# Cross-attention on one core: a hint instruction for the closing branch of the batch loop on every engine

## What is computed

```python
Q = (q @ Wq + bq).reshape(b, s, H, DH).transpose(0, 2, 1, 3)
K = (k @ Wk + bk).reshape(b, s, H, DH).transpose(0, 2, 1, 3)
V = (v @ Wv + bv).reshape(b, s, H, DH).transpose(0, 2, 1, 3)
scores = jnp.einsum('bhqd,bhkd->bhqk', Q, K) / jnp.sqrt(jnp.float32(DH))
scores = scores * mask
attn = jax.nn.softmax(scores, axis=-1)
ctx = jnp.einsum('bhqk,bhkd->bhqd', attn, V)
ctx = ctx.transpose(0, 2, 1, 3).reshape(b, s, H * DH)
x = q + ctx @ Wo + bo
out = (x - mean(x)) * rsqrt(var(x) + LN_EPS) * gamma + beta
```

## Time and profile before

| | us |
|---|---|
| median of 3 runs | 2252.9 (2248.44 to 2253.84) |
| the profiled execution, its own time | 2253.91 |
| its span, first to last instruction | 2252.1 |
| PE busy | 2119.7 (94%) |
| DVE busy | 1933.0 (86%) |
| ACT busy | 1782.9 (79%) |
| POOL busy | 1038.0 (46%) |

### The profile page before, as it was taken

The page is one execution under the profiler, slowest core; times in us unless marked ns, Lnnn a source line. Parts: engine busy times, 40 slices in busy tenths (PEclk is TensorE's granted clock), DMA queues, the critical chain, the costliest instruction groups (busy, mean ns, idle before and its releaser), DMA issues.

```text
span 2252.1 us, 46384 instructions
## 1 busy us (share of the span) xinstructions
PE 2119.7 (94%) x12348; PEld 886.9 (39%) x12348; DVE 1933.0 (86%) x4283; ACT 1782.9 (79%) x3809; POOL 1038.0 (46%) x1576
## 2 busy tenths in 40 slices
PE   2699999999999999999999999999999999999985
PEld 1234444444444344444444444443444434444432
DVE  6779988898988898888989888898988888988882
ACT  3579798887969879697887969788796978879781
POOL 2116263463726436273543726355372634537234
PEclk8799999999999999999999999999999999999997
DMA  6359789697887969789697868969697896968783
GB/s 219 70 118 177 161 155 206 129 191 142 174 182 145 197 131 187 152 168 195 130 196 141 184 145 171 194 133 194 142 183 157 159 203 129 192 140 176 143 157 87
DMA packets 1117594, 363.28 MB, mean 161 GB/s; under 512 B 1073504, under 2 KB 1073504, under 8 KB 1117408
## 3 DMA queue, kind: packets, MB, share of 16 engines
q1 hardware_dynamic: 1114288, 361.58, 78.2%
q10 hardware_dynamic: 3120, 0.01, 0.1%
HBM read 76.30 MB, written 16.78 MB: 41 GB/s over the span
## 4 chain that ended last, share of the span: by engine, by line
PE 75%; issue 8%; POOL 7%; DVE 6%; ACT 2%; DMA 1%; POOLq 0%; DVEq 0%; ACTq 0%; SPq 0%
PE fill_ps L396 17%; PE fill_ps L397 16%; PE fill_ps L398 16%; PE score_ps L449 13%; PE ctx_ps L470 11%; POOL raw L1199 3%; DVE score_ps L923 2%; ACT probs L621 1%; DVE p L937 1%; POOL bk_scaled L1215 1%; DVE small L805 1%; POOL neg_max L1222 1%; DVE k L952 1%; ACT p L635 1%; POOL cT L1205 1%
## 5 line engine op out<-in xcount | busy, mean ns | idle before, releaser
L621 ACT ACTIVATE probs<-score_ps,neg_max 128x512 f32<-128x512 f32 x1024 | 695.8, 693 | 187.3 <-POOL neg_max L1222 181.7
L923 DVE CUSTOM_DVE_ANT_0 score_ps<-score_ps,mask_sb,small 128x512 f32<-128x512 f32 x1024 | 723.6, 753 | 93.6 <-PE score_ps L449 89.6
L635 ACT ACTIVATE p<-probs,inv_sum 128x512 f16<-128x512 f32 x1024 | 675.0, 724 | 132.9 <-DVE inv_sum L931 92.2
L937 DVE SCALAR_TENSOR_TENSOR p<-probs,inv_sum,p 128x512 f16<-128x512 f32 x896 | 677.6, 792 | 47.9 <-issue 38.1
L1222 POOL TENSOR_SCALAR neg_max<-row_max 128x2 f32<-128x2 f32 x512 | 142.4, 278 | 681.1 <-DVE row_max L923 664.7
L449 PE MATMUL score_ps<-k,q 64*128 64x512 f16 x3072 | 397.8, 380 | 15.3 <-ACT probs L621 8.9
L470 PE MATMUL ctx_ps<-pT,v 128*64 128x512 f16 x3072 | 359.8, 384 | 18.6 <-DMA pT<-p 15.6
L1228 POOL TENSOR_SCALAR down_sum<-row_sum 128x4 f32<-128x4 f32 x256 | 67.9, 265 | 393.9 <-ACT probs L621 385.5
L470 PEld LDWEIGHTS ctx_ps<-pT,v 128*64 128x64 f16 x3072 | 165.7, 110 | 205.4 <-issue 72.5
L449 PEld LDWEIGHTS score_ps<-k,q 64*128 64x128 f16 x3072 | 129.9, 94 | 263.8 <-ACT probs L621 80.9
L396 PE MATMUL fill_ps<-wv,cT 128*128 128x512 f16 x512 | 197.4, 385 | 31.6 <-DVE k L952 25.8
(11 more groups left out here) (91 smaller groups left out, 2992.0 us busy)
## 6 DMA issues: line engine op xcount, KB each, us to landing
raw<-in_xt SPq DMA_DIRECT2D x64, 256.0 KB, 3.2
raw<-in_ct SPq DMA_DIRECT2D x64, 256.0 KB, 3.2
mask_sb<-in_mask_Bx1xSxS_fk SPq DMA_DIRECT2D x64, 256.0 KB, 3.2
acc<-in_x SPq DMA_DIRECT2D x64, 256.0 KB, 3.0
out<-acc SPq DMA_DIRECT2D x64, 256.0 KB, 2.4
pT<-p SPq DMA_TRANSPOSE x512, 4.5
wq_staged<-in_L_xattn_Wq SPq DMA_DIRECT2D x4, 512.0 KB, 7.1
wk_staged<-in_L_xattn_Wk SPq DMA_DIRECT2D x4, 512.0 KB, 10.7
```

The source lines that it names most:

```text
L621: nc.scalar.activation(probs[:, i % E_TILES, :], score_ps[:, i % 4, :], ACT.Exp, bias=neg_max[:, p % 2, i:i + 1], accum_out=row_sum[:, p % ...
L635: nc.scalar.activation(p16[:, q, a, 0, :], probs[:, i % E_TILES, :], ACT.Copy, scale=inv_sum[:, p % 2, i:i + 1]).then_inc(p_rounded, 1)
L923: nc.vector.tensor_tensor_reduce(out=score_ps[:, i % 4, :], in0=score_ps[:, i % 4, :], in1=mask_sb[:, q, :], scale=score_scale, scalar=-3. ...
L937: nc.vector.scalar_tensor_tensor(out=p16[:, q, a, 1, :], in0=probs[:, i % E_TILES, :], scalar=inv_sum[:, p % 2, i:i + 1], in1=p16[:, q, a, ...
```

## The change

Each engine's loop is built by the same loop helper, now with an option that puts one more instruction, a branch prefetch hint, first in the body. It names the closing compare-and-branch of that engine's loop and so its target, the top of the body. It is executed in every one of the 14 iterations, on all five engines. Nothing else in the program is different.

```diff
--- before.py
+++ after.py
@@ -219,7 +219,7 @@
         def batches(eng, body):
             body(None, None, 0, False)
             body(None, 0, 1, True)
-            with eng.Fori(1, B - 1) as b:
+            with nc.Fori(1, B - 1, engines=bass.OrderedEngineSet([eng.engine]), hint_back_edge=True) as b:
                 body(b - 1, b, b + 1, False)
             body(B - 2, B - 1, None, False)
             body(B - 1, None, None, False)
```

## The result

| | before | after |
|---|---|---|
| median, us | 2252.89 (2248.44 to 2253.84) | 2214.93 (2214.65 to 2215.35) |
| span of the profiled execution | 2252.1 | 2213.3 |
| V4 to V4, one iteration | 132.60, three of 13 at 134.0 to 134.4 | 130.06 |
| code packets of q14, whole span | 167 | 24 |

The ratio is 0.9832, with a 95% interval of 0.9819 to 0.9844: 38 us less. The forecast was 2223 with a range of 2218 to 2246.

What follows compares the result with a forecast made beforehand. PE was taken to bound the kernel, idling at each loop jump while DVE and ACT fetched code. From the profiled 2253.9 us, 25.8 of PE waits and 4.9 of clock loss came off, hint 0: 2223.2, stated as 2223, range 2218 to 2246.

## What to carry to other kernels

In a hand-written loop, search every engine's rows for waits that come once per iteration on the loop's first line (here the bodies of 390 and 472 instructions had them, those of 196 and 245 did not), and also once per iteration anywhere else, whatever releaser the profile names; the hint belongs at the top of the body, on the engines whose rows show it, and not on the others. Size a stall by comparing the lengths of the same block in stretches with and without it, since overlapping matmul records hide 0.16 us of each gap and more of several small ones. An edit can change how often the clock falls behind the same waits, so compare the granted clocks beside the times. If the code may grow, writing the loop out is better still here: 2203 us, with waits on constants.

## What the runs showed of the hardware

- With the hint at the top, DVE jumps back over a body of 473 instructions with no gap; a hint two instructions ahead of the branch does nothing (2252.46 us).
- Without a hint DVE and ACT load code in the loop even where the body fits the two blocks it is placed in (123 packets, ten per iteration); with it, none, or five per iteration that nobody waits for.
- Code comes in packets of 128 instructions on DVE and ACT and of 256 on PE (127 and 257 instructions per packet in the kernel without a loop).
- PE streams straight-line code from memory (98 packets of 16 KB) without a stop in the iterations, but with the hint at the top of its loop it stops 0.9 to 1.2 us at the exit.
- A 2 us pause of PE can cost 1.7 us more through the clock: the granted clock fell to the 1.2 GHz level behind three of 13 such pauses in one kernel and six in another. The kernel with the hint on ACT alone lost in this way the 5 us that its edit had won (mean granted clock 0.9776 against 0.9799).
